# Attention loop of a graph network: ScalarE loads a body's number once and stages four bodies ahead, one exponential gives weights and kept factor, messages overwrite the products

## What is computed

```
q = (nfeat @ Wq.T).reshape(n, HEADS, HEAD_DIM) / SCALING
k = (nfeat @ Wk.T).reshape(n, HEADS, HEAD_DIM)
v = (nfeat @ Wv.T).reshape(n, HEADS, HEAD_DIM)
attn = einsum('ehd,ehd->eh', k[src], q[dst]) + attn_bias
m = segment_max(attn, dst);  a = exp(attn - m[dst])
s = segment_sum(a, dst);     a = a / s[dst]
out = segment_sum(v[src] * a[:, :, None], dst)
return out.reshape(n, FEAT) @ Wo.T
```

## Time and profile before

| what | us |
|---|---|
| median of 3 executions | 4425.66 |
| profiled execution, its own time | 4438.98 |
| its span, first to last instruction | 4437.5 |
| POOL busy over the span | 1418.9 |
| VectorE busy | 2545.3 |
| TensorE busy (matmul) | 3031.0 |
| ScalarE busy | 1118.0 |
| granted TensorE clock, mean | 0.829 |

### The profile page before, as it was taken

One profiled execution on the slowest core, in us unless ns is written; L12 is line 12 of the kernel. 1 busy time (PEld: TensorE's weight loads), 2 busy tenths in 40 slices (PEclk: granted clock), 3 DMA queues, 4 the chain that ended last, 5 costly groups with the idle time before them and its releaser, 6 DMA issues. The chain is left out here.

```text
span 4437.5 us, 49631 instructions
## 1 busy us (share of the span) xinstructions
PE 3031.0 (68%) x14277; PEld 2242.9 (51%) x14277; DVE 2545.3 (57%) x4638; ACT 1118.0 (25%) x2246; POOL 1418.9 (32%) x1393
## 2 busy tenths in 40 slices
PE   4234554545454543884888858999967996699598
PEld 2111211112121222663888856777746885588487
DVE  7457777877777745344999963111134666233333
ACT  1111111111111102220455533333324552000122
POOL 4666666666666624343600000000000000001233
PEclk8667667766777675996999977999988998799799
DMA  2466666666666644343444442000037443655333
GB/s 93 151 188 191 194 193 196 195 198 192 195 197 193 191 129 162 66 68 90 175 177 177 177 174 75 12 12 12 6 101 141 143 134 107 243 176 184 101 66 53
DMA packets 289833, 613.00 MB, mean 138 GB/s; under 512 B 52204, under 2 KB 195696, under 8 KB 279760
## 3 DMA queue, kind: packets, MB, share of 16 engines
q0 software_dynamic: 105584, 294.01, 24.5%
q1 hardware_dynamic: 166800, 267.12, 17.5%
q10 hardware_dynamic: 17360, 50.80, 3.8%
HBM read 437.46 MB, written 176.95 MB: 138 GB/s over the span
## 5 line engine op out<-in xcount | busy, mean ns | idle before, releaser
L2056 PE MATMUL gnn_p_msg<-gnn_msg,gnn_ident 128*128 128x512 f32 x928 | 673.6, 893 | 764.6 <-DVE gnn_msg L2144 414.8
L2009 POOL DMA_INDIRECT gnn_got<-kv,gnn_index x928 | 880.0, 948 | 455.4 <-issue 304.5
L2056 PEld LDWEIGHTS gnn_p_msg<-gnn_msg,gnn_ident 128*128 128x128 f32 x928 | 258.9, 293 | 1178.7 <-issue 1149.8
L2525 PE MATMUL tables_p_pair<-tables_spread,tables_hot 128*128 128x100 f32 x3328 | 398.9, 279 | 20.2 <-DVE tables_spread L2499 16.8
L2525 PEld LDWEIGHTS tables_p_pair<-tables_spread,tables_hot 128*128 128x128 f32 x3328 | 384.6, 194 | 34.2 <-DVE tables_spread L2499 30.2
L2130 DVE TENSOR_TENSOR gnn_prod<-gnn_got,gnn_p_both 128x2048 f32<-128x2048 f32 x116 | 265.4, 2288 | 225.4 <-issue 173.8
L746 DVE SCALAR_TENSOR_TENSOR ffn_acc<-ffn_pC,ffn_gates,ffn_acc 128x256 f32<-128x256 f32 x200 | 88.9, 480 | 395.7 <-PE ffn_pC L597 395.7
L2806 PE MATMUL gnn_p_sum<-gnn_hs,gnn_edge 128*128 x2500 | 288.9, 278 | 32.2 <-DVE gnn_edge L2836 32.0
L2144 DVE TENSOR_TENSOR gnn_msg<-gnn_got,gnn_p_both 128x2048 f32<-128x2048 f32 x116 | 264.7, 2282 | 74.3 <-ACT gnn_p_both L2037 43.5
L2806 PEld LDWEIGHTS gnn_p_sum<-gnn_hs,gnn_edge 128*128 128x128 f32 x2500 | 285.4, 194 | 37.0 <-issue 36.2
L1150 PE MATMUL ffn_pA<-ffn_hw,ffn_slabs 128*128 128x256 f32 x1250 | 274.3, 381 | 33.8 <-DMA ffn_beta<-in_L_ffn_beta 33.8
(11 more groups left out here) (417 smaller groups left out, 4551.3 us busy)
## 6 DMA issues: line engine op xcount, KB each, us to landing
weight_table<-tables_weight_slab SPq DMA_DIRECT2D x13, 3200.0 KB
count_table<-tables_count_row SPq DMA_DIRECT2D x13, 3200.0 KB
ffn_slabs<-weight_table SPq DMA_DIRECT2D x25, 1600.0 KB, 7.1
gnn_cell<-count_table ACTq DMA_DIRECT2D x50, 576.0 KB, 3.8
state<-gnn_out SPq DMA_DIRECT2D x116, 136.0 KB
ffn_xs<-by_expert SPq DMA_DIRECT2D x60, 260.0 KB, 3.3
gnn_got<-kv,gnn_index POOLq DMA_INDIRECT x928
ffn_x<-x SPq DMA_DIRECT2D x20, 640.0 KB, 5.6
```

The source lines that it names most:

```text
L2009: pool.indirect_dma_start(out=got[k][:, r, :], out_offset=None, in_=kv_dram, in_offset=rows_at(index[k][:, r:r + 1])).then_inc(gathered[k] ...
L2056: last = nc.tensor.matmul(p_msg[k][:], ident[:], msg[k][:, r:r + 2].rearrange("p r h d -> p (r h d)"), start=(r == 0), stop=(r == R - 2))
L2525: last = nc.tensor.matmul(at, hot[c % AHEAD][:, r, :], spread[c % AHEAD][:, r, :], start=True, stop=True)
```

## The change

- ScalarE loads `piece_of[b + 4]` once a body and uses it for the index and for the staging. Staging is for body b+4 now, as the index was; before the loop four bodies are staged instead of one. `prod` and `p_q` have four buffers instead of two.
- One exponential over the 64 shifted scores and the 8 shifted old peaks writes weights and kept factor to PSUM, `p_exp[k]`. The activations of lines 2041 and 2042 and the buffers `keep` and `weight` go. VectorE reads both from PSUM in `keep_part`.
- `msg[k]` is the product part of `prod[k]`: the messages overwrite the products, so TensorE reads rows of 32 numbers with one number between them.
- The semaphore `keep_ready` becomes `peak_carried`, raised by the copy of the peak; TensorE's wait for `keep_ready` goes, as does VectorE's behind the loop. VectorE waits before the loop for all four stagings.
- PSUM: four banks of `p_msg` as before, two for queries and two for exponentials, where there were two for both.

The diff, cut to its core:

```diff
@@ -1916,14 +1916,12 @@
         all_got = s.sb("got", [P, SETS, R, 2 * F])
         got = [all_got[:, k] for k in range(SETS)]
         index = [s.sb(f"index{k}", [P, R], i32) for k in range(SETS)]
-        prod = [s.sb(f"prod{v}", [P, R, HEADS, HD + 1]) for v in range(2)]
-
-        msg = [s.sb(f"msg{k}", [P, R, HEADS, HD]) for k in range(SETS)]
-        weight = [s.sb(f"weight{k}", [P, R, HEADS]) for k in range(SETS)]
+        prod = [s.sb(f"prod{k}", [P, R, HEADS, HD + 1]) for k in range(SETS)]
+
+        msg = [prod[k][:, :, :, 0:HD] for k in range(SETS)]
         weight_sum = s.sb("weight_sum", [P, HEADS])
 
         score = [s.sb(f"score{v}", [P, R + 1, HEADS]) for v in range(2)]
-        keep = [s.sb(f"keep{k}", [P, HEADS]) for k in range(SETS)]
         out = [s.sb(f"out{k}", [P, STATE]) for k in range(SETS)]
         peak = [out[k][:, MSG:STATE] for k in range(SETS)]
         ident = s.sb("ident", [P, P])
@@ -1939,9 +1937,12 @@
         piece_of = s.sb("piece_of", [P, ALL_BODIES], i32)
         groups = s.sb("groups", [P, 1], i32)
         p_msg = [s.ps(f"p_msg{k}", [P, 512]) for k in range(SETS)]
-        p_both = [s.ps(f"p_both{v}", [P, 512]) for v in range(2)]
-        p_q = [p_both[v][:, 0:F] for v in range(2)]
-        p_weight = [p_both[v][:, F:F + R * HEADS] for v in range(2)]
+        q_bank = [s.ps(f"q_bank{v}", [P, 512]) for v in range(2)]
+        exp_bank = [s.ps(f"exp_bank{v}", [P, 512]) for v in range(2)]
+        p_q = [q_bank[k % 2][:, k // 2 * F:(k // 2 + 1) * F] for k in range(SETS)]
+        p_exp = [exp_bank[k // 2][:, k % 2 * 256:k % 2 * 256 + (R + 1) * HEADS] for k in range(SETS)]
+        p_weight = [p_exp[k][:, 0:R * HEADS] for k in range(SETS)]
+        p_keep = [p_exp[k][:, R * HEADS:(R + 1) * HEADS] for k in range(SETS)]
         const_loaded = s.sem("const_loaded")
         number_set = s.sem("number_set")
         plan_ready = s.sem("plan_ready")
@@ -1953,7 +1954,7 @@
         staged = s.sem("staged")
         shifted = s.sem("shifted")
         weights_ready = s.sem("weights_ready")
-        keep_ready = s.sem("keep_ready")
+        peak_carried = s.sem("peak_carried")
         summed = s.sem("summed")
         out_ready = s.sem("out_ready")
         stored = s.sem("stored")
@@ -1989,7 +1990,7 @@
                     pool.sem_inc(released[k], 1)
                 pool.sem_inc(stored, 16 * SETS)
                 pool.sem_inc(summed, LAG)
-                pool.sem_inc(keep_ready, 1)
+                pool.sem_inc(peak_carried, 1)
                 for k in range(TILES):
                     pool.indirect_dma_start(out=q[:, k, :], out_offset=None, in_=q_dram,
                                             in_offset=rows_at(perm[:, k, NODE:NODE + 1])).then_inc(q_loaded, 16)
@@ -2014,34 +2015,31 @@
                 def piece(b):
                     return act.value_load(piece_of[0:1, bass.ds(b, 1)], min_val=0, max_val=TILES * MAIN - 1)
 
-                def find_index(b, k):
-                    at = piece(b)
+                def find_index(at, k):
                     act.activation(index[k][:], source[:, bass.ds(at * R, R), 0], ACT.Copy).then_inc(index_ready, 1)
 
-                def stage(b, v):
-
-                    at = piece(b)
-                    act.activation(p_q[v].rearrange("p (a n) -> p a n", a=1), q[:, bass.ds(at // MAIN, 1), :],
+                def stage(at, k):
+
+                    act.activation(p_q[k].rearrange("p (a n) -> p a n", a=1), q[:, bass.ds(at // MAIN, 1), :],
                                    ACT.Copy, scale=SCALE)
-                    act.activation(prod[v][:, :, :, HD], bias[:, bass.ds(at * R, R), 1:EDGE], ACT.Copy).then_inc(staged, 1)
+                    act.activation(prod[k][:, :, :, HD], bias[:, bass.ds(at * R, R), 1:EDGE], ACT.Copy).then_inc(staged, 1)
 
                 act.wait_ge(plan_ready, 1)
                 for k in range(SETS):
-                    find_index(k, k)
+                    find_index(piece(k), k)
                 act.wait_ge(q_loaded, 16 * TILES)
-                stage(0, 0)
+                for k in range(SETS):
+                    stage(piece(k), k)
                 with act.Fori(0, group_count(act)) as g:
                     for k in range(SETS):
                         b, v = g * SETS + k, k % 2
                         act.wait_ge(shifted, b + 1)
-                        act.activation(p_weight[v], score[v][:, 0:R, :].rearrange("p r h -> p (r h)"),
-                                       ACT.Exp).then_inc(weights_ready, 1)
-
-                        act.activation(score[1 - v][:, R, :], peak[k], ACT.Identity, bias=first[:, bass.ds(b + 1, 1)])
-                        act.activation(keep[k][:], score[v][:, R, :], ACT.Exp)
-                        act.activation(weight[k][:], score[v][:, 0:R, :], ACT.Exp).then_inc(keep_ready, 1)
-                        stage(b + 1, 1 - v)
-                        find_index(b + SETS, k)
+                        act.activation(p_exp[k], score[v][:].rearrange("p r h -> p (r h)"), ACT.Exp).then_inc(weights_ready, 1)
+                        act.activation(score[1 - v][:, R, :], peak[k], ACT.Identity, bias=first[:, bass.ds(b + 1, 1)])\
+                            .then_inc(peak_carried, 1)
+                        at = piece(b + SETS)
+                        find_index(at, k)
+                        stage(at, k)
 
             @block.tensor
             def _(pe):
@@ -2051,10 +2049,9 @@
                     for k in range(SETS):
                         b = g * SETS + k
                         pe.wait_ge(released[k], g + 2)
-                        pe.wait_ge(keep_ready, b + 2)
                         for r in range(0, R, 2):
-                            last = nc.tensor.matmul(p_msg[k][:], ident[:],
-                                                    msg[k][:, r:r + 2].rearrange("p r h d -> p (r h d)"),
+                            last = nc.tensor.matmul(p_msg[k][:].rearrange("p (r h d) -> p r h d", r=2, h=HEADS), ident[:],
+                                                    msg[k][:, r:r + 2],
                                                     start=(r == 0), stop=(r == R - 2))
                         last.then_inc(summed, 1)
 
@@ -2069,10 +2066,9 @@
                     dve.memset(score[0][:, R, :], -BIG)
                     for k in range(SETS):
                         dve.memset(out[k][:], 0.0)
-                        dve.memset(keep[k][:], 0.0)
                     for k in range(SETS - LAG, SETS):
                         dve.memset(p_msg[k][:], 0.0)
-                        dve.memset(weight[k][:], 0.0)
+                        dve.memset(p_exp[k], 0.0)
                     dve.drain()
                     dve.tensor_tensor_scan(ends[:], ones[:], main_bodies[:], 0.0, ALU.mult, ALU.add)
                     dve.drain()
@@ -2102,9 +2098,9 @@
 
                 def keep_part(k):
 
-                    dve.tensor_reduce(weight_sum[:], weight[k % SETS][:].rearrange("p r h -> p h r"), AX.X, ALU.add)
+                    dve.tensor_reduce(weight_sum[:], p_weight[k % SETS].rearrange("p (r h) -> p h r", h=HEADS), AX.X, ALU.add)
                     dve.tensor_tensor(by_head(out[k % SETS]), by_head(out[(k - 1) % SETS]),
-                                      over(keep[k % SETS][:], [P, HEADS, HD + 1], "p (h a) -> p h a", a=1), ALU.mult)
+                                      over(p_keep[k % SETS], [P, HEADS, HD + 1], "p (h a) -> p h a", a=1), ALU.mult)
 
                 def add_sums(k, count):
 
@@ -2119,6 +2115,7 @@
                     last.then_inc(out_ready, 1)
 
                 plan()
+                dve.wait_ge(staged, SETS)
                 with dve.Fori(0, group_count(dve)) as g:
                     for k in range(SETS):
                         b, v = g * SETS + k, k % 2
@@ -2127,13 +2124,13 @@
                         wide = [P, R, HEADS, HD]
                         dve.wait_ge(gathered[k], g * (16 * R) + 16 * R)
                         dve.wait_ge(staged, b + 1)
-                        dve.tensor_tensor(prod[v][:, :, :, 0:HD], keys,
-                                          over(p_q[v], wide, "p (a h d) -> p a h d", a=1, h=HEADS), ALU.mult)
+                        dve.tensor_tensor(prod[k][:, :, :, 0:HD], keys,
+                                          over(p_q[k], wide, "p (a h d) -> p a h d", a=1, h=HEADS), ALU.mult)
                         dve.drain()
                         dve.tensor_reduce(score[v][:, 0:R, :].rearrange("p r h -> p (r h)"),
-                                          prod[v][:].rearrange("p r h d -> p (r h) d"), AX.X, ALU.add)
+                                          prod[k][:].rearrange("p r h d -> p (r h) d"), AX.X, ALU.add)
                         dve.drain()
-                        dve.wait_ge(keep_ready, b + 1)
+                        dve.wait_ge(peak_carried, b + 1)
                         dve.wait_ge(stored, 16 * b + 16)
                         dve.tensor_reduce(peak[k], score[v][:].rearrange("p r h -> p h r"), AX.X, ALU.max)
```

(5 more changed lines are left out.)

## The result

The changed kernel takes 4450.94 us (median of 6, 4440.70 to 4456.28) against 4422.49 us (4421.70 to 4426.33) for the kernel before: a ratio of 1.0059, 95% interval [1.0044, 1.0074]. It is slower by 28 us, where 89 us less were forecast.

What follows compares the result with a forecast made beforehand. The prediction took ScalarE's and SyncE's queue instructions per body to bound the attention loop. One load fewer cuts a body from 11.66 to 10.9 us, 89 us over 115 steps, other parts 0: 4336 us, range 4245 to 4396.

Steps and rivals of the forecast that it cites:

- the balance: Attention loop: 22.7 ScalarE and SyncE queue instructions a body, 1.43 per us plus 3.6 per us of POOL's rest.
- I take 0: TensorE's sums in the loop: messages overwriting products add no wait of VectorE for them, 0 us.
- The terms of no weight: Loop parts other than the single load: staging ahead, one exponential, PSUM reads, messages over products, each counted at 0.
- Staging ahead: ScalarE's copies for body b+4: moves VectorE's wait from line 2130 to 2144, counted at 0, between 0 and 23.2 us.
- POOL's floor of 10.0 us: POOL in the loop: 8 gathers a body, 1.25 us apart back to back, need 10.0 us a body.
- Rival 2: Loop: short rests of POOL don't fill the store; at worst 13.1 us a body, 4596 us; chance 0.10, 0.05 of it slower.
- Rival 1: Loop: the queue keeps up, choking becomes rare, POOL's 10.0 us a body rules: 191 us less, 4235 us; chance 0.20.
- Rival 3: TensorE's matmuls pay for reading gapped rows; at twice the median, 2.11 us each, 5024 us; chance 0.02.
- Rival 4: Queues are choked only in the recorded run, so timed runs don't change: 4426 us; chance 0.02.

Runs made afterwards that it cites:

- e1: Changed kernel with ScalarE loading the body's number twice again, both four bodies ahead: 4418.33 us, ratio 0.9989 to the kernel before.
- e3: Changed kernel with SyncE storing only every fourth body's state and no queue instructions for the others: 4441.91 us, ratio 1.0040 to the kernel before.
- e4: Changed kernel with POOL gathering only 4 of a body's 8 edges: 4199.17 us (one execution).
- e18: Changed kernel with 8 gathers a body of rows of 256 numbers instead of 512: 4457.80 us (one execution); kernel before beside it 4430.5 us.
- e17: Changed kernel with 4 matmuls a body instead of 8: 4399.66 us (one execution); kernel before beside it 4430.5 us.
- e2: Changed kernel with staging for the next body again, with its own load; merged exponential and messages over products stay: 4417.00 us, ratio 0.9985 to the kernel before.
- e9: Changed kernel, unaltered, on a chip where no queue was choked: 4215.43 us against 4217.06 us for the kernel before, ratio 0.9997.
- e14: Changed kernel with three loads of the number a body, one unused, where no queue was choked: 4218.12 us, ratio 0.9998 to the kernel before.

## Why the prediction was wrong

**The observation held, the law made of it did not.** Queues at 0.70 us, on a common grid, with POOL's rests as the relief: all of this is in the profile after as well. The step that failed is the balance, "22.7 = 1.43 x 11.66 + c x 1.66", with its conclusion that what counts is "the number of queue instructions per body". It fitted one number with one free constant. e1 (3.0 more a body on that line, 26 us less) and e3 (three quarters of SyncE's gone, loop 2 us shorter where 1160 to 1180 us were expected) both refute it. The rate of 1.43 per us is what the queues get while something else is full, not a store that they empty.

**What fills the path is the gathers** (e4), by their number and not their bytes (e18), as far as these single executions show. A body has 8, whatever ScalarE does. With eight, POOL rested in every run on a choked chip: 152 us in e17, 165 and 166 us in e1 and e2, 173 us before, 187 us after, 207 us in e18 (idle time between gathers beyond 0.30 us, in rests over 0.5 us). The loop's length goes with these rests and not with ScalarE's instructions, so taking instructions from its queue did not bring the 89 us, and nothing tried there or in SyncE's queue came near POOL's 10.0 us a body.

**The second failed step is "I take 0" for TensorE's sums**: "VectorE has waited for TensorE's sums of it two bodies before that, so no wait is added" and "VectorE waited only 2.1 us for TensorE's sums". That 2.1 us was small although the signals were late already (15 of 68 prompt, by e9's count above); ScalarE stopped POOL and VectorE first, as e1 and e2 suggest. I had written that an engine off the path still frees or holds others, and asked of each wait what is late next, but only among ScalarE's own copies: I named line 2144 as the place to which the wait would move. It went to line 2117, on TensorE's signal, which no view of the profile before showed to be late. In VectorE's account the waits before the product and the messages, 173.8 + 23.2 + 43.5 us and 30.9 us more under "issue", 271 us together, became 48.8 + 206 + 17.5 + 16.6 = 289 us. The profiled loops differ by 10.7 us, the medians by 28 us. That TensorE's instructions are what makes its signals hold VectorE is shown by e17, in one execution; how the second load prevents it is argued.

**The terms of no weight were right.** The merged exponential, the reads from PSUM and the gapped messages cost nothing (e2): the multiply is 420 ns after and 423 ns before, the weight sum 217 against 259 ns, the matmul's median 1.057 us in both. Staging ahead is 0 (e1 against e2). Loads and queue instructions are 124 (120 forecast) and 488 (460 forecast). A load of the number takes 0.28 us in the median even where nothing is choked (e9), not the 0.2 us that the prediction let hold there. POOL's floor of 10.0 us was exact (e9: 1150.2 / 115 = 10.0 us).

**The rivals.** Rival 2 gave the right side with 0.05, but by another mechanism: rests did not become short and frequent, they became rare and long (20 waits of 9 us for VectorE in place of 29 of 5.2 us for ScalarE). Rival 1's time, 4235 us, is close to what both kernels take on a clear chip (4215 and 4217 us), which the change does not bring about. Rival 3 is out: no matmul got longer. Rival 4 I had dismissed by comparing the medians with the profiled execution. That argument was empty: each timed execution has a span and a granted clock of its own, so each must have been recorded too. Behind this stands the sentence of the Trainium skill (NOTIFIC — the notification-queue block, The write path) on an internal pipeline that holds producers back; a path filled by the number of gathers and of TensorE's instructions would suit it. The counts above fit as well: each gather raises its semaphore 16 times, whatever its bytes, so e18 asks for as many rises as the changed kernel (2750 kept in the trace) and e4 for half (9041 kept, and 113 of TensorE's 116). That speaks for the recording of the rises, or the rises themselves, as what a choked chip can't carry. No run here shows which, because none was taken without its record, and so none shows whether a kernel that nobody records would be choked at all.

**What stays open.** What differs between choked and clear chips; whether the choking would be there without the record; what exactly a gather puts on the path; and whether a rest by hand would serve a choked chip. The 11 us for which VectorE waits, until POOL has run out of free buffers, were seen and not explained further. e4, e17 and e18, on which the part of gathers and matmuls rests, are one execution each.

The version to keep is e2: merged exponential and messages over products, with staging as before. On a choked chip it takes 4417.0 us, 0.15% less than the kernel before and 0.74% less than the changed one; on a clear chip it wasn't run, and the changed kernel and e14 suggest no difference.

## What to carry to other kernels

When queue instructions or signals are late at a constant grid and several engines show it, the cause is shared, and taking work from one victim moves the wait to the next: look for what the late stretches have in common (here the number of indirect gathers in a row) and halve that first, in an experiment, before counting anybody's instructions. A wait of 2 us may be small only because another brake comes before it. Look at which instruction of a line waits before giving the wait a name: in e17 it was the second addition, not the one that waits for the sums. And run the kernel before beside each variant: here the chip was worth 5%, eight times the change.

## What the runs showed of the hardware that was not expected

- Back-to-back indirect gathers of 128 rows (1.25 us each) went with slow sequencer instructions of ScalarE and SyncE, 0.70 us and more in place of 0.04 to 0.28 us, on some chips and not on others: 4422 against 4217 us for one and the same kernel.
- TensorE's completion signal came about 27 us after the end of its last matmul by the trace (915.9 to 943 us), when POOL stopped issuing. With half as many matmuls (e17) no addition waited for it.
- On the choked chips the trace kept 2750 to 3040 rises of semaphores in the loop (9041 with half of the gathers), on the clear ones about 17550.
- Half of the bytes per gather brought nothing (loop 1374.7 us), half of the gathers cleared the queues (1102.4 us).
- A drain on POOL behind a small memset, right after a gather, took nearly 4 us.
